# The causal mask of an attention added to the scores by a matrix product instead of a vector addition

## The chip, the core and the metric

The kernel runs on one core of a Trainium2 chip. TensorE is called PE here, VectorE DVE, ScalarE ACT and GpSimd POOL. The metric is the device time of one execution in microseconds; less is better.

## The reference

Four layers, each applied to a layer-normed input and added back: an attention, a gated feed-forward network with integer weights, a state-space layer and a small per-head MLP. The change lies in the attention. It has 2 sequences of 512 tokens, 16 query heads in groups of 4 on 4 key heads, head size 64:

```python
scores = jnp.einsum('bhqd,bhkd->bhqk', q, kg) * scale
causal = jnp.tril(jnp.ones((S, S), dtype=bool))
scores = jnp.where(causal[None, None], scores, jnp.finfo(scores.dtype).min)
attn = jax.nn.softmax(scores, axis=-1)
out = jnp.einsum('bhqk,bhkd->bhqd', attn, vg)
```

## The kernel before

The program is one after the other: `attention`, `feed_forward`, `state_space`, `head_mlp`, each closed by a stage end at which all engines meet. `attention` has three blocks: projections and the first convolution; the second convolution with the rotary embedding; and the block that the change touches, from line 745 on. All its data are fp32.

That last block begins with turning q and k by PE transposes (L763), copied from PSUM by ACT (L838). `k_twice` holds each key head twice, so that `kt` has it on partitions 0 to 63 and again on 64 to 127. A query head h lies in `qt` on partitions 0 to 63 when h is even and on 64 to 127 when it is odd.

Then comes the loop over 32 units (b, z, kv): sequence b, query block z of 128 tokens, counted down from 3 to 0, key head kv. A unit has four heads (GQ = 4), and since later key blocks are masked off its scores have (z + 1) * 128 columns, so 512, 384, 256 or 128. Units 0 to 15 are sequence 0, units 16 to 31 sequence 1. PSUM bank i (0 to 3) holds the scores of head i of the unit, banks 4 and 5 the turned probabilities, bank 6 the value products, bank 7 the output projection.

In step u each engine does this, in the order of its own program:
- PE: `scores(u)`, one product for each of four heads (L775), each after the exponentials of the same head in unit u - 1 have freed the bank (`exp_done`); at odd u `values` for two older units (L798); from u = 7 on a quarter of an output projection (`project`, L815); `turn(u - 1)`, four transposes for each key block of the unit before (L787), where block k waits until ACT has emptied the bank that block k - 2 used (`pt_done`).
- DVE: for each head `top`: wait for the product, add the mask block `neg` in PSUM to the last 128 columns (L868), take the row maximum (L872); and `invert`, the reciprocal of the row sum (L880); then the copies of the value products (L891) and, every fourth step, the layer norm of the projection.
- ACT: four exponentials with row sums (L849), then the copies of the turned probabilities of unit u - 1 (L858).
- POOL: the probabilities times the reciprocal (L922).

`neg` is 128 x 128: 0 on and below the diagonal, -3.0e38 above it. It is loaded in the first block, as `core.ident` is, the identity.

Of the kernel before, what the change touches and what calls it, by code (L numbers as in the profile page):

```python
# [5 lines left out]
ALU = mybir.AluOpType  # L6
ACT = mybir.ActivationFunctionType
AX = mybir.AxisListType
F32 = mybir.dt.float32
F32R = mybir.dt.float32r  # L10
# [3 lines left out]
P = 128  # L14
B, S, D = 2, 512, 512
# [157 lines left out]
def add_vector(dve, core, s, t, src, scaled):  # L173

    dve.bn_stats(core.stats[:, t, :], src).then_inc(s.stats, 1)
    dve.wait_ge(s.stats, t + 1)
    dve.bn_aggr(core.mv[:, t, :], core.stats[:, t, :]).then_inc(s.aggr, 1)
    dve.wait_ge(s.aggr, t + 1)
    dve.tensor_scalar(core.vare[:, t:t + 1], core.mv[:, t, 1:2], LN_EPS, None, ALU.add).then_inc(s.vare, 1)
    dve.wait_ge(s.rstd, t + 1)  # L180
    if t >= 2:
        dve.wait_ge(s.added, t - 1)
    dve.tensor_scalar(scaled[:, t % 2, :], src, core.mv[:, t, 0:1], core.rstd[:, t:t + 1],
                      ALU.subtract, ALU.mult).then_inc(s.scaled, 1)
# [11 lines left out]
def attention(core, x_in, w_qkv, w_o, w_c1q, w_c1k, b_c1, w_c2q, w_c2k, b_c2q, b_c2k, key_temp,  # L196
              c_ident, c_neg, c_sel, c_cos, c_sin):
    nc, ps, x = core.nc, core.ps, core.x
# [4 lines left out]
    with ExitStack() as outer:  # L203
        def keep(name, shape, dt=F32):
            return outer.enter_context(nc.sbuf_tensor(name, shape, dt))
# [4 lines left out]
        neg = keep("neg", [P, P])  # L210


        with ExitStack() as inner:
            def sb(name, shape, dt=F32):
                return inner.enter_context(nc.sbuf_tensor(name, shape, dt))
# [483 lines left out]
        with ExitStack() as inner:  # L699
# [7 lines left out]
            kt = sb("kt", [P, KV0, B * S])  # L707
# [5 lines left out]

            ot = q_tok[:, :, :, :].rearrange("p t h d -> p (t h d)").rearrange("p (f n) -> p f n", f=QT)
            scaled = sb("scaled", [P, 2, D])

            twice_done = core.sem("a_twice_done")
            turn_ready = core.sem("a_turn_ready")
            turn_done = core.sem("a_turn_done")
            sc_ready = core.sem("a_sc_ready")  # L720
            masked = core.sem("a_masked")
            max_done = core.sem("a_max_done")
            exp_done = core.sem("a_exp_done")
            rsum_done = core.sem("a_rsum_done")
# [19 lines left out]
            with nc.Block() as blk:  # L744
# [5 lines left out]
                def _(pe):  # L750
                    for t in range(NT):
                        for j in range(TURNS):
                            n = t * TURNS + j
# [9 lines left out]
                                last = pe.transpose(ps[:, n % 4, i * P:(i + 1) * P], src, core.ident[:, :])  # L763
                            last.then_inc(turn_ready, 1)
                    pe.wait_ge(turn_done, NT * TURNS)

                    def scores(u):
                        b, z, kv = units[u]
                        wide = (z + 1) * P
                        for i in range(GQ):  # L770
                            h = kv * GQ + i
                            at = slice((h % 2) * HD, (h % 2 + 1) * HD)
                            if u >= 1:
                                pe.wait_ge(exp_done, (u - 1) * GQ + i + 1)
                            pe.matmul(ps[:, i, 0:wide], qt[at, h // 2, b * S + z * P:b * S + (z + 1) * P],  # L775
                                      kt[at, kv, b * S:b * S + wide], start=True, stop=True).then_inc(sc_ready, 1)

                    def turn(u):
                        b, z, kv = units[u]
# [49 lines left out]

                @blk.scalar  # L830
                def _(act):
                    for t in range(NT):
                        for j in range(TURNS):
                            n = t * TURNS + j
                            at = t // 2 * 2 * P + t % 2
                            dst = qt[:, 4 * j:4 * j + 4, at:at + 2 * P - 1:2] if j < TURNS - 1 else kt[:, :, t * P:(t + 1) * P]
                            act.wait_ge(turn_ready, n + 1)
                            act.activation(dst, ps[:, n % 4, :].rearrange("p (i n) -> p i n", i=4), ACT.Copy).then_inc(turn_done, 1)  # L838
                    for u in range(NU + 1):
                        if u < NU:  # L840
                            b, z, kv = units[u]
                            wide = (z + 1) * P
                            for i in range(GQ):
                                n = u * GQ + i
                                act.wait_ge(max_done, n + 1)
                                if u >= 2:
                                    act.wait_ge(pt_ready, tiles_before[u - 1])
                                    act.wait_ge(prob_done, n - 2 * GQ + 1)
                                act.activation(prob[:, u % 2, i, 0:wide], ps[:, i, 0:wide], ACT.Exp,  # L849
                                               bias=nmax[:, u % 2, i:i + 1],  # L850
                                               accum_out=psum_row[:, u % 2, i:i + 1]).then_inc(exp_done, 1)
                        if u >= 1:
                            for k in range(units[u - 1][1] + 1):
                                n = tiles_before[u - 1] + k
                                act.wait_ge(pt_ready, n + 1)
                                if u >= 5:
                                    act.wait_ge(pv_ready, (u - 5) // 2 + 1)
                                act.activation(prob_t[:, (u - 1) % 4, k, :, :],  # L858
                                               ps[:, 4 + n % 2, :].rearrange("p (i n) -> p i n", i=GQ), ACT.Copy).then_inc(pt_done, 1)

                @blk.vector
                def _(dve):
                    def top(u, i):
                        b, z, kv = units[u]
                        n = u * GQ + i
                        own = ps[:, i, z * P:(z + 1) * P]
                        dve.wait_ge(sc_ready, n + 1)
                        dve.tensor_tensor(own, own, neg[:, :], ALU.add).then_inc(masked, 1)  # L868
                        dve.wait_ge(masked, n + 1)
                        if u >= 2:  # L870
                            dve.wait_ge(exp_done, n - 2 * GQ + 1)
                        dve.tensor_reduce(nmax[:, u % 2, i:i + 1], ps[:, i, 0:(z + 1) * P], AX.X, ALU.max,  # L872
                                          negate=True).then_inc(max_done, 1)

                    def invert(u, i):
                        n = u * GQ + i
                        dve.wait_ge(exp_done, n + 1)
                        if u >= 2:
                            dve.wait_ge(prob_done, n - 2 * GQ + 1)
                        dve.reciprocal(rsum[:, u % 2, i:i + 1], psum_row[:, u % 2, i:i + 1]).then_inc(rsum_done, 1)  # L880

                    def store(pair):

                        b, z, first_kv = units[2 * pair]
                        t = b * ZB + z
                        dve.wait_ge(pv_ready, pair + 1)
                        for half in range(2):
                            kv = first_kv + half
                            turned = ps[half * HD:(half + 1) * HD, PV_BANK, :].rearrange("p (f e n) -> p f e n", e=2, n=P)
                            for e in range(2):  # L890
                                dve.tensor_copy(ot[e * HD:(e + 1) * HD, kv * (GQ // 2):(kv + 1) * (GQ // 2), t * P:(t + 1) * P],  # L891
                                                turned[:, :, e, :]).then_inc(ot_done, 1)

                    def add(j):
                        t = order[j]
                        dve.wait_ge(wo_ready, j + 1)
                        add_vector(dve, core, ad, j, ps[:, OUT_BANK, :], scaled)

                    for e in range(2):
                        dve.tensor_copy(k_twice[:, :, :, e, :], k_tok[:, :, :, :]).then_inc(twice_done, 1)  # L900
                    for u in range(NU + KV0 + LAG):
                        for i in range(GQ):
                            if u < NU:
                                top(u, i)
                                if i >= 1:
                                    invert(u, i - 1)
                        if u < NU:
                            invert(u, GQ - 1)
                        if u % 2 == 1 and 3 <= u < NU + 3:
                            store((u - 3) // 2)  # L910
                        if u >= KV0 + LAG and (u - KV0 - LAG) % KV0 == KV0 - 1:
                            add((u - KV0 - LAG) // KV0)
# [1452 lines left out]
```

## Time and profile before

| | us |
|---|---|
| median of 3 runs | 2778.62 |
| lowest and highest run | 2778.03, 2780.35 |
| the profiled execution | 2781.88 |
| its span | 2780.1 |
| mean granted clock of TensorE in it | 0.953 of full speed |

| engine | busy us | share of the span |
|---|---|---|
| PE | 2493.9 | 90% |
| DVE | 1750.2 | 63% |
| ACT | 1411.5 | 51% |
| POOL | 1506.0 | 54% |

The loop of the last attention block takes some 228 us of the span, from 468 to 697 us; the state-space layer takes most of the rest. The trace gives an fp32 product as two matmul records and an fp32r product as one. Matmul records overlap when they are pipelined, since each lasts until its result is out, so it is the distance between two starts that tells how long PE is taken up. A time is read from the start of the span.

### The profile page before, as it was taken

What the parts mean: (1) busy time and instruction counts of PE and PEld (TensorE: products, weight loads), DVE (VectorE), ACT (ScalarE), POOL (GpSimd) and SP (SyncE); (2) the same over time, 40 slices, a digit from 0 to 9 for tenths busy, and PEclk for the clock granted to TensorE, in tenths of its full rate; (3) what the DMA queues carried; (4) which work ended last, traced back from release to release, by engine and by line L of the source; (5) the groups of instructions that cost most, each with busy time, mean ns of one, the idle gap of its engine ahead of it and who ended that gap; (6) DMA issues with size and microseconds to landing.
All of it is one profiled execution on the core that took longest, in us unless ns stands there. A gap on an engine that the chain in (4) does not pass through costs nothing. (4 is left out here: it accounts for less than half of the span.)

```text
span 2780.1 us, 37283 instructions
## 1 busy us (share of the span) xinstructions
PE 2493.9 (90%) x12664; PEld 1826.8 (66%) x12664; DVE 1750.2 (63%) x3126; ACT 1411.5 (51%) x2787; POOL 1506.0 (54%) x1291
## 2 busy tenths in 40 slices
PE   7989995898799359999999999999999999999948
PEld 3464443444587247877877877877877877877734
DVE  2153444566423547778778778778777777777764
ACT  2200003554221156766866866866766766766603
POOL 0053465444001026777777777767767767767641
PEclk9999997999899679999999999999999999999978
DMA  4012310000210053334333333333343343343210
GB/s 157 0 56 62 118 47 30 1 1 1 91 39 0 34 181 102 111 114 115 111 114 122 113 116 125 104 115 122 106 124 114 102 131 107 102 136 108 70 46 31
DMA packets 142188, 241.86 MB, mean 87 GB/s; under 512 B 28209, under 2 KB 48433, under 8 KB 141745
## 3 DMA queue, kind: packets, MB, share of 16 engines
q1 hardware_dynamic: 142000, 239.48, 27.7%
q8 instruction: 103, 1.69, 0.3%
q14 instruction: 85, 0.69, 0.1%
HBM read 232.08 MB, written 7.34 MB: 86 GB/s over the span
## 5 line engine op out<-in xcount | busy, mean ns | idle before, releaser
L1646 ACT ACTIVATE mix<-mix,sc 128x128 f32<-128x128 f32 x1024 | 310.8, 389 | 4.4 <-DMA mix<-row_cum 4.4
L96 PE MATMUL ps<-s_xt_hi,w_in_hi 128*128 128x512 f32 x640 | 267.0, 417 | 49.4 <-ACT sg L1638 32.5
L1745 DVE SCALAR_TENSOR_TENSOR feat<-ps,chan,feat 128x511 f32<-128x511 f32 (+2 forms) x384 | 283.9, 739 | 10.0 <-ACT feat L1628 8.2
L1857 POOL TENSOR_TENSOR w_in_lo<-w_in_raw,w_in_hi 128x512 fp32r<-128x512 f32 x160 | 216.6, 1354 | 114.8 <-ACT w_in_hi L1603 114.8
L1775 DVE TENSOR_TENSOR y_lo<-y,y_hi 128x512 fp32r<-128x512 f32 x128 | 171.4, 1339 | 161.5 <-ACT y_hi L1662 159.5
L1734 DVE TENSOR_TENSOR mix<-mix,cb 128x512 f32<-128x512 f32 x256 | 271.0, 1064 | 0.0
L1841 POOL TENSOR_TENSOR xend<-xdt,sc 128x384 f32<-128x384 f32 x128 | 106.9, 835 | 283.8 <-DVE xdt L1708 282.2
L98 PE MATMUL ps<-s_xt_hi,w_in_lo 128*128 128x512 f32 x640 | 253.2, 396 | 0.0
L97 PE MATMUL ps<-s_xt_lo,w_in_hi 128*128 128x512 f32 x640 | 251.8, 394 | 0.0
L96 PE MATMUL ps<-s_xt_hi,w_g_hi 128*128 128x512 f32 x512 | 213.1, 416 | 21.1 <-DVE feat L1745 21.0
L1518 PE MATMUL ps<-w_o_hi,y_hi 128*128 128x512 f32 x512 | 207.4, 405 | 5.4 <-DVE y_lo L1775 3.4
L98 PE MATMUL ps<-s_xt_hi,w_g_lo 128*128 128x512 f32 x512 | 204.0, 398 | 0.0
L1520 PE MATMUL ps<-w_o_hi,y_lo 128*128 128x512 f32 x512 | 203.3, 397 | 0.0
L1519 PE MATMUL ps<-w_o_lo,y_hi 128*128 128x512 f32 x512 | 203.0, 396 | 0.0
L97 PE MATMUL ps<-s_xt_lo,w_g_hi 128*128 128x512 f32 x512 | 201.4, 393 | 0.0
L1853 POOL TENSOR_TENSOR y<-y,sg 128x512 f32<-128x512 f32 x128 | 195.1, 1524 | 10.0
L1862 POOL TENSOR_TENSOR w_g_lo<-w_g_raw,w_g_hi 128x512 fp32r<-128x512 f32 x128 | 199.0, 1555 | 0.0
L1628 ACT ACTIVATE feat<-ps,chan 128x512 f32<-128x512 f32 x128 | 98.4, 769 | 183.1 <-PE ps L98 183.1
L1708 DVE TENSOR_TENSOR xdt<-ps,sc 128x512 f32<-128x512 f32 x128 | 88.1, 688 | 161.1 <-PE ps L1543 160.8
L1874 POOL TENSOR_TENSOR y_sq_sum<-y_sq_sum,y_sq 128x512 f32<-128x512 f32 x112 | 166.8, 1489 | 8.8
L96 PEld LDWEIGHTS ps<-s_xt_hi,w_in_hi 128*128 128x128 f32 x640 | 121.7, 190 | 75.3 <-issue 54.0
L1850 POOL TENSOR_TENSOR y<-y,off 128x384 f32<-128x384 f32 x128 | 129.7, 1013 | 65.3 <-DVE off L1727 65.3
(261 smaller groups left out, 5970.2 us busy)
## 6 DMA issues: line engine op xcount, KB each, us to landing
mix<-row_cum SPq DMA_DIRECT2D x128, 512.0 KB, 5.8
w_in_raw<-in_w_conv_in SPq DMA_DIRECT2D x160, 256.0 KB, 3.2
w_g_raw<-in_w_gate_in SPq DMA_DIRECT2D x128, 256.0 KB, 3.5
ecb<-row_ecum SPq DMA_DIRECT2D x256, 96.0 KB, 3.4
w_o_raw<-in_w_out SPq DMA_DIRECT2D x64, 256.0 KB, 3.0
w<-in_w_c2q SPq DMA_DIRECT2D x16, 768.0 KB, 4.8
w<-in_w_c2q SPq DMA_DIRECT2D x16, 512.0 KB, 3.8
wqkv<-in_w_qkv SPq DMA_DIRECT2D x1, 3072.0 KB, 13.6
```

The lines of the kernel that those rows point to most:

```text
L96: pe.matmul(out, a_hi, b_hi, start=(n == 0), stop=False)
L97: pe.matmul(out, a_hi, b_lo, start=False, stop=False)
L98: last = pe.matmul(out, a_lo, b_hi, start=False, stop=(n == len(terms) - 1))
L1518: pe.matmul(ps[:, OUT + z, :], a_hi, w_o_hi[:, i, :], start=(i == 0), stop=False)
L1519: pe.matmul(ps[:, OUT + z, :], a_hi, w_o_lo[:, i, :], start=False, stop=False)
L1520: last = pe.matmul(ps[:, OUT + z, :], a_lo, w_o_hi[:, i, :], start=False, stop=(i == GT - 1))
L1646: last = act.activation(m, m, ACT.Relu, bias=sc[:, b, CUM, z, 2 * i + e:2 * i + e + 1], scale=-1.0)
L1734: last = dve.tensor_tensor(m, m, cb[:, :], ALU.mult)
L1745: dve.scalar_tensor_tensor(out=to, in0=ps[:, j % 2, 0:S - back], scalar=chan[:, bb % B, j, K1 - 1 - back:K1 - back], in1=to, op0=ALU.mult, ...
L1853: pool.tensor_tensor(yt, yt, sg[:, gate_at(g, bb, i), :], ALU.mult).then_inc(s["y_done"], 1)
L1857: pool.tensor_tensor(w_in_lo[:, n % RING, :, :], w_in_raw[:, n % RING, :, :], w_in_hi[:, n % RING, :, :].bitcast(F32), ALU.subtract).then_ ...
L1862: pool.tensor_tensor(w_g_lo[:, i % RING, :, :], w_g_raw[:, i % RING, :, :], w_g_hi[:, i % RING, :, :].bitcast(F32), ALU.subtract).then_inc ...
```

## The change

The mask is no longer added by DVE. Each score product is left open (`stop=False`), and a second product, identity times mask block, is accumulated on its last 128 columns. Both its operands are fp32r copies, made by ACT at the start of the block. DVE's addition, its semaphore `masked` and the wait on it go; DVE takes the maximum when the mask product is done. PE waits once for the two copies.

```diff
+            neg_r = sb("neg_r", [P, P], F32R)
+            ident_r = sb("ident_r", [P, P], F32R)
+            mask_ready = core.sem("a_mask_ready")
-            masked = core.sem("a_masked")
@@ PE, before the loop
                     pe.wait_ge(turn_done, NT * TURNS)
+                    pe.wait_ge(mask_ready, 2)
@@ PE, scores(u), for each head i
                             pe.matmul(ps[:, i, 0:wide], qt[at, h // 2, b * S + z * P:b * S + (z + 1) * P],
-                                      kt[at, kv, b * S:b * S + wide], start=True, stop=True).then_inc(sc_ready, 1)
+                                      kt[at, kv, b * S:b * S + wide], start=True, stop=False)
+                            pe.matmul(ps[:, i, z * P:(z + 1) * P], ident_r[:, :], neg_r[:, :],
+                                      start=False, stop=True).then_inc(sc_ready, 1)
@@ ACT, at the start of the block
+                    act.activation(neg_r[:, :], neg[:, :], ACT.Copy).then_inc(mask_ready, 1)
+                    act.activation(ident_r[:, :], core.ident[:, :], ACT.Copy).then_inc(mask_ready, 1)
@@ DVE, top(u, i)
-                        own = ps[:, i, z * P:(z + 1) * P]
                         dve.wait_ge(sc_ready, n + 1)
-                        dve.tensor_tensor(own, own, neg[:, :], ALU.add).then_inc(masked, 1)
-                        dve.wait_ge(masked, n + 1)
```

## Rows read from the trace of the kernel before

**Rows 1.** Stretches, all engines: busy us and instructions each, PEclk, DMA share, GB/s.
```profile
468.00:575.00 107.00, 89.47 (x396) 44.81 (x397) 65.46 (x223) 59.91 (x167) 48.37 (x66) 0.89 0.00 1
575.00:682.00 107.00, 97.45 (x449) 48.53 (x449) 74.92 (x249) 61.85 (x172) 53.57 (x74) 1.00 0.00 1
```

**Rows 2.** Groups by line and shape, 468 to 697 us: busy us, mean ns, idle before.
```profile
L868 DVE TENSOR_TENSOR ps<-ps,neg 128x128 f32<-128x128 f32 x128 | 36.6, 286 | 52.0 <-PE ps L775 51.8
```

**Rows 3.** PE's waits, 468 to 697 us: us in total, times, longest.
```profile
PE ps L787 <- ACT prob_t L858: 19.8, 16, 3.2
PE ps L815 <- DVE scaled L183: 5.0, 3, 2.8
```

**Rows 4.** Timeline of PE alone: start us, lasting us, what, idle before it.
```profile
471.64 4.04 PE L775 MATMUL ps<-kt,qt 64*128 64x512 f32 x8 [1.06 <-ACT prob L849]
...
481.80 3.79 PE L775 MATMUL ps<-kt,qt 64*128 64x512 f32 x8
...
579.27 3.94 PE L775 MATMUL ps<-kt,qt 64*128 64x512 f32 x8
...
588.50 1.99 PE L775 MATMUL ps<-kt,qt 64*128 64x512 f32 x8
...
594.96 1.14 PE L787 MATMUL ps<-ident,prob 128*128 128x128 f32 x8 [1.69 <-ACT prob_t L858]
...
604.64 1.15 PE L787 MATMUL ps<-ident,prob 128*128 128x128 f32 x8 [0.25 <-ACT prob_t L858]
605.72 1.56 PE L775 MATMUL ps<-kt,qt 64*128 64x384 f32 x8
...
660.94 0.84 PE L775 MATMUL ps<-kt,qt 64*128 64x128 f32 x4
...
663.64 1.94 PE L798 MATMUL ps<-prob_t,v_tok 128*64 128x512 f32 x8 [0.58 <-ACT prob_t L858]
```

**Rows 5.** Timeline of DVE and ACT in unit 18, and ACT's first copy of the block.
```profile
453.97 0.65 ACT L838 ACTIVATE qt<-ps 128x512 f32<-128x512 f32 x1 [12.87 <-PE ps L763]
...
589.65 0.30 DVE L868 TENSOR_TENSOR ps<-ps,neg 128x128 f32<-128x128 f32 x1 [0.90 <-PE ps L775]
589.99 0.69 DVE L872 TENSOR_REDUCE nmax<-ps 128x1 f32<-128x512 f32 x1
...
590.71 0.69 ACT L849 ACTIVATE prob<-ps,nmax 128x512 f32<-128x512 f32 x1 [1.51 <-DVE nmax L872]
...
593.64 0.69 ACT L849 ACTIVATE prob<-ps,nmax 128x512 f32<-128x512 f32 x1 [0.21 <-DVE nmax L872]
...
594.32 1.08 ACT L858 ACTIVATE prob_t<-ps 128x512 f32<-128x512 f32 x2
```

**Rows 6.** Timeline of PE and its weight loads (PEld) in short windows of unit 18.
```profile
588.29 0.27 PE L787 MATMUL ps<-ident,prob 128*128 128x128 f32 x1
588.50 0.70 PE L775 MATMUL ps<-kt,qt 64*128 64x512 f32 x2
588.49 0.30 PEld L775 LDWEIGHTS ps<-kt,qt 64*128 64x128 f32 x4 [0.17 <-issue]
589.03 0.19 PEld L775 LDWEIGHTS ps<-kt,qt 64*128 64x128 f32 x2 [0.24 <-issue]
589.46 0.19 PEld L775 LDWEIGHTS ps<-kt,qt 64*128 64x128 f32 x2 [0.24 <-issue]
...
590.41 0.30 PEld L815 LDWEIGHTS ps<-wo,q_tok 128*128 128x128 f32 x2 [0.76 <-issue]
590.95 0.19 PEld L815 LDWEIGHTS ps<-wo,q_tok 128*128 128x128 f32 x1 [0.24 <-issue]
```

**Rows 7.** Timeline of PE, fp32r products of 512 columns in the feed-forward layer.
```profile
780.12 0.39 PE L97 MATMUL ps<-f_xt_lo,f_w_hi 128*128 128x512 f32 x1
780.35 0.39 PE L98 MATMUL ps<-f_xt_hi,f_w_lo 128*128 128x512 f32 x1
```

**Rows 8.** A stretch in batch 0, columns as in rows 1.
```profile
481.80:485.50 3.70, 3.70 (x9) 1.18 (x8) 1.52 (x4) 1.13 (x2) 0.00 (x0) 0.50 0.00 0
```

## The prediction, made before the change was run

> **What bounds the kernel now.** I read the table of stretches first, then the groups of the attention loop, then the timeline of TensorE (PE) and the waits. The softmax loop of the attention runs from about 468 to 697 us of a span of 2780.1 us; the change touches nothing after it. In its first half, batch 0, PE is busy 89.5 of 107 us at a mean clock of 0.89; in its second half, batch 1, 97.5 of 107 us at full clock [rows 1]. DVE is busy 65 and 75 us. So PE is nearly the bound in batch 1, and DVE's addition, 36.6 us in all [rows 2], is not work that all runs on the path. The loop has 32 units (2 batches, 4 query blocks, 4 key heads), each with 4 heads. A unit on PE is: score products; in some units value products; in most an output projection part; then the turning of the previous unit's probabilities. The third turn (k=2) needs PSUM bank 4 back, which ACT empties only after the four exponentials of the present unit. Where that chain (scores, addition, maximum, exponential, four times, then the copy) is longer than PE's own work, PE stands still in front of L787: 19.8 us in 16 waits [rows 3]. In unit 18 (batch 1, four key blocks) it is the 1.69 us before 594.96 [rows 4]. The chain there: addition at 589.65, maximum 0.34 later, first exponential at 590.71, the fourth at 593.64, copy at 594.32, turn at 594.96 [rows 4, 5]. In units with value products the wait is 0.25 us, the mere exchange of two banks (the unit that ends at 605.72) [rows 4].
>
> **How the score products run now.** This is what the change meets. A head's product uses 64 rows of the array, the even heads rows 0 to 63, the odd ones 64 to 127. An fp32 product is two passes. At 588.50 two matmuls begin together and last 0.70 us as a pair, with four weight loads beside them; the next pairs begin at 589.03 and 589.46 [rows 6]. So two heads run at the same time, a pass of 512 columns taking 0.43 us for both, and four heads take 1.91 us (588.50 to 590.41) where one after another they would take eight passes, 3.4 us. For 384 columns the eight recorded passes last 1.56 us against 1.99 [rows 4]; the four pairs save 0.43 us, a pass 0.107 per 128 columns. So a pass takes 0.32, 0.215 and 0.11 us for 384, 256 and 128 columns.
> The same rows price a switch between 64-row and 128-row products. The last pass begins at 589.89 (0.43 after 589.46), the projection's first load at 590.41: 0.52 and not 0.43. Its next load but one comes 0.54 later, again 0.11 too much. PE's weight port sat idle 0.76 us on "issue" before it [rows 6]. The way in is alike: transpose at 588.29, scores at 588.50 (0.21, where a transpose pass is 0.11: eight last 1.14 at 594.96, less 0.27 for the last and 0.10 for the opening load, by seven [rows 4]), the second pass 0.53 later. Both ways the extra is 0.10 + 0.10 = 0.20 us, made of a drain and a weight load that is not hidden.
> The page "TensorEngine Tiling (Array Packing)" of the Trainium skill, section Key Properties, says that changing the tiling mode drains TensorE; the trace agrees with 0.20 us. Without such a drain, by the order of the products alone, the sum below would be half of the switches lower, some 20 us.
>
> **The change, part by part.**
> 1. *Removed:* 128 additions on DVE, 0.286 us each [rows 2], and their wait. Worth at most 0.34 us in front of a unit's first maximum, and about 0.25 per further head where DVE paces (four exponentials from 590.71 to 593.64 are about 1.0 apart, of which ACT itself needs 0.68: from 593.64 to the copy at 594.32) [rows 5].
> 2. *Added on PE:* 128 products identity x mask, 128 rows, 128 columns, between the products of two heads. No row shows an fp32r product of 128 columns. A pass of 512 fp32r columns starts every 0.23 us [rows 7], a quarter of which is 0.057; the transposes of the same shape in fp32 take the 0.11 a pass of above, 0.22 for both. I take m = 0.11, the same shape, and keep 0.057 and 0.22 as ends.
> 3. *Changed by it:* the order is now head 0 (rows 0 to 63), mask (all rows), head 1 (rows 64 to 127), mask. PE runs its products in order, and the mask product holds all rows, so head 1 cannot run beside head 0. The scores stretch becomes 8 passes one after another, 4 m, 7 switches of 0.20 and the opening load 0.10. For 512 columns: 3.43 + 0.44 + 1.37 + 0.10 = 5.34 us, where 1.91 was: +3.43. For 384, 256, 128 columns by the same sum: +3.00, +2.57, +2.14. Eight units of each: +89 us of PE time.
> 4. *What of this PE's idle time takes up.*
> (a) Before L787: 19.8 us. The new chain for 512 columns without projection: the last mask product begins 5.23 after the unit's start and is recorded for 0.27 like a transpose [rows 6], so it ends at 5.50; then come maximum to exponential 0.72, exponential to copy 0.68, copy to turn 0.64 [rows 4, 5]. That is 7.54, where PE is free at 5.34 + 0.97 (eight transpose passes of 0.11 and the half switch); so 1.2 us stay idle in two early units, an estimated 1.0 in two of 384 columns, whose maximum and exponential are shorter, and 0.25 in eleven or twelve others. 7.5 stay, 12.3 are taken up.
> (b) PE's other waits, which now lie behind the longer scores stretch: 1.1 us before 471.64 and 2.1 in the 4.04 there, 2.0 in the 3.94 at 579.27 (score products that wait for the exponentials of the unit before); in each batch's unit like that at 660.94, whose value products begin 2.7 us later where 0.64 would do, 2.1, twice [rows 4]; two of the three waits for DVE in front of L815, 2.2 [rows 3]; and an estimated 1.5 of small ones beside them. Together 13.1.
> (c) The clock. In batch 0 it was at 1.2 GHz of 2.4 in several stretches, after PE had stood up to 3.2 us [rows 3]; there the score products last 3.79 us at 481.80 instead of 1.99 [rows 4, 8]. By the stretches this costs about 10 us. With the change the early gaps are 1.0 to 1.2 us, like the 1.69 us of unit 18, after which the clock stayed up. I take it that most of it goes.
> Sum: 89 - 12.3 - 13.1 = 63.6 with the clock as it was, 53.6 with it up all the way. I take +55, near the second.
> 5. *Two ACT copies and two waits* at the loop's front: ACT stands idle 12.87 us before its first copy at 453.97 [rows 5], and each new one has a quarter of that copy's columns and so takes no more than its 0.65 us. Nothing; at most 1.3 us if that cover were gone. The removed semaphore frees nothing else. What follows the loop (feed-forward, state space) is fenced off by a stage end and only starts later.
> Sum against the profiled execution: 2781.9 (span 2780.1 and 1.8 around it) + 55 = 2837. The median of the runs is 3.3 us lower, so 2778.6 + 55 = 2834.
>
> **Rivals.**
> A. *Pairs survive and no switch is paid* (the other side). If PE can load the identity beside running 64-row products and still start head 1 at once, only m is added. Chain-bound units gain 1.1 us at 512 columns, 1.0 at 384, 0.6 at 256: some 11 us over about a dozen units; each head in the 15 PE-bound units costs m, and once in the others: 11.2 - 70 m. That is -7 us (2772) at m = 0.057, -3.5 at 0.11, zero at 0.16, +4 at 0.22. It needs weights to pass from one mode to the other without the 0.76 us that the weight port idles [rows 6], so little speaks for it.
> B. *The clock falls instead.* In the new scores stretch the array streams only 0.97 of 1.37 us per head at 512 columns, 0.33 of 0.72 at 128, half of the rows at a time. If that holds the clock at 1.2 GHz as idle time did in batch 0, the 10 us stay and each added 3.0 to 3.4 us in some seven early units doubles: 63.6 + 21, with m at its upper end + 12: up to +97, 2875.
> C. *The switch costs half:* only the load, not the drain, since the mask needs no data from outside. 7 x 0.10 x some 28 units = 20 us less, with the small m 6 less: +27 to +35, 2806 to 2814.
> D. *The change does nothing measurable:* DVE's addition is hidden and so is the product. It would need case A with m near 0.11 to 0.2.
>
> **How the numbers follow.** Forecast (about +40 to +75) 0.70; B 0.15; C 0.08; A and D together 0.07, of which 0.03 faster by over 0.2% (5.6 us, about what a measurement can tell from no change) and 0.04 within it. Slower by more: 0.93. Ends of m alone move the sum by -6 and +12 us, the clock by -2 and +8. The range goes from C's 2805 to 2880, just beyond B, and leaves out A and D and some of B.
>
> **What the profile would show.** Right: L775's two heads no longer begin together; the stretch from a unit's first score product to the next other work is about 5.3 us at 512 columns and 2.8 at 128; PEld idles on "issue" twice per head; the wait of L787 for ACT shrinks to some 8 us; ACT's exponentials are spaced 1.3 to 1.4 us at 512 columns instead of 1.0; DVE waits longer for PE. Batch 1, 575 to 682 us before, takes 34 us more; batch 0 some 20 more; everything after is only moved. Wrong: score products still beginning in pairs (A), a mean clock below 0.89 in the loop (B), switches of 0.1 us (C), or a stretch that differs because a 128-column fp32r product is nearer 0.06 or 0.22 than 0.11.

## The result, and the profile after

| | us |
|---|---|
| before, median of 5 runs | 2779.63 (2778.03 to 2780.93) |
| after, median of 5 runs | 2860.53 (2839.75 to 2863.03) |
| ratio | 1.0276 (95% interval 1.0241 to 1.0312) |
| the profiled execution after, and its span | 2839.75, 2837.9 |
| mean granted clock in it, and in the other four | 0.954, and 0.943 to 0.945 |

The change makes the kernel 2.8% slower, 81 us, where 55 were forecast, with a range up to 2880 us. The profiled execution is the fastest of the five, 21 us below their median, so the profile after shows less than the median costs.

The table of stretches, for batch 0 (first score product of unit 0 to that of unit 16) and 15 units of batch 1 (unit 16 to unit 31), columns as in rows 1; here and below these stretches begin up to 0.4 us behind the product itself. In the kernel before:

```profile
468.59:575.00 106.41, 89.46 (x396) 44.80 (x397) 65.46 (x223) 59.37 (x165) 48.37 (x66) 0.89 0.00 1
575.00:670.86 95.86, 88.28 (x415) 44.13 (x414) 67.57 (x224) 58.00 (x160) 49.39 (x66) 1.00 0.00 1
```

In the changed kernel:

```profile
468.54:600.71 132.17, 127.74 (x461) 62.18 (x461) 52.49 (x164) 60.01 (x167) 49.21 (x68) 0.91 0.00 1
600.71:735.58 134.87, 132.86 (x474) 63.44 (x473) 53.56 (x161) 59.20 (x160) 49.58 (x66) 0.94 0.00 1
```

PE is busy 128 and 133 us instead of 89 and 88, DVE 52 and 54 instead of 65 and 68. DVE was relieved of 13 or 14 us in each, and PE took on 38 and 45. The timeline of PE alone shows how, in a unit of 512 columns (unit 19, with value products and a projection part):

```profile
629.29 1.12 PE L778 MATMUL ps<-kt,qt 64*128 64x512 f32 x2
630.34 0.33 PE L780 MATMUL ps<-neg_r,ident_r 128*128 128x128 f32 x1
630.60 1.12 PE L778 MATMUL ps<-kt,qt 64*128 64x512 f32 x2
631.65 0.33 PE L780 MATMUL ps<-neg_r,ident_r 128*128 128x128 f32 x1
631.90 1.12 PE L778 MATMUL ps<-kt,qt 64*128 64x512 f32 x2
632.96 0.33 PE L780 MATMUL ps<-neg_r,ident_r 128*128 128x128 f32 x1
633.21 1.12 PE L778 MATMUL ps<-kt,qt 64*128 64x512 f32 x2
634.27 0.33 PE L780 MATMUL ps<-neg_r,ident_r 128*128 128x128 f32 x1
634.52 3.65 PE L803 MATMUL ps<-prob_t,v_tok 128*64 128x512 f32 x16
```

Before, one row held the eight passes of all heads in 1.99 us [rows 4], two heads side by side [rows 6]. Now each head stands alone: two passes, mask product, 1.31 us later the next head, and 5.23 us until the value products where it was 1.92 in the same unit. The weight loads (PEld) of the same unit say what stands between:

```profile
630.34 0.19 PEld L780 LDWEIGHTS ps<-neg_r,ident_r 128*128 128x128 f32 x1 [0.76 <-issue]
630.60 0.29 PEld L778 LDWEIGHTS ps<-kt,qt 64*128 64x128 f32 x2
631.65 0.19 PEld L780 LDWEIGHTS ps<-neg_r,ident_r 128*128 128x128 f32 x1 [0.76 <-issue]
```

The idle weight port in front of a load, 0.76 us on "issue", is the one that stood in front of L815 in unit 18 [rows 6], once per unit, behind its score products. Now it stands in front of each mask product: in these rows the identity is loaded only when the mask product begins, not beside the 64-row products before it. ACT paces with PE, no longer with DVE; the exponentials of unit 18 are 1.31 us apart, from 1.00:

```profile
622.15 0.69 ACT L856 ACTIVATE prob<-ps,nmax 128x512 f32<-128x512 f32 x1 [1.44 <-DVE nmax L876]
...
623.46 0.69 ACT L856 ACTIVATE prob<-ps,nmax 128x512 f32<-128x512 f32 x1 [0.53 <-DVE nmax L876]
...
624.78 0.69 ACT L856 ACTIVATE prob<-ps,nmax 128x512 f32<-128x512 f32 x1 [0.53 <-DVE nmax L876]
```

The waits, all engines (who waited for whom, us in total, times, longest), show DVE's maximum waiting for PE 120 us in all; PE's wait for ACT is down from 19.8 us [rows 3] to 6.4:

```profile
DVE nmax L876 <- PE ps L780: 120.3, 113, 14.9
...
PE ps L792 <- ACT prob_t L865: 6.4, 16, 1.2
```

### The profile page after: what moved, and what is told of

Same layout as the page of the kernel before. It is cut to its first block and busy times, and to the rows that moved or that the text cites. A ratio compares the mean times of both kernels' runs of the same rounds, so it can differ in the third digit from the quotient of the medians.

```text
span 2837.9 us, 37414 instructions
## 1 busy us (share of the span) xinstructions
PE 2571.2 (91%) x12792; PEld 1860.2 (66%) x12792; DVE 1721.4 (61%) x2998; ACT 1413.4 (50%) x2789; POOL 1506.7 (53%) x1291
## 5 line engine op out<-in xcount | busy, mean ns | idle before, releaser
L926 POOL TENSOR_TENSOR prob<-prob,rsum 128x512 f32<-128x512 f32 (+3 forms) x128 | 91.3, 719 | 174.0 <-DVE rsum L884 173.1
```

## The experiments

In the runs below the kernel before was run beside each; its median there was 2775.7 to 2776.8 us. The diffs are against the changed kernel unless said, and shortened. The granted clock has two levels here, 1.00 and half of it; "at half clock" is the time at the lower one, which is twice what is missing to 1.00 in a stretch's mean, times its length.

### Where the changed kernel's scatter comes from: `again` and `again2`

No edit.

> The changed kernel once more, unchanged. Its profiled execution took 2839.75 us, the four others 2857 to 2863, and their mean granted clock was 0.944 instead of 0.954. Theory: the work on every engine is the same, and the 20 us are stretches at 1.2 GHz; a profile near 2860 us then shows the same distances of 1.31 us between two heads of 512 columns wherever the clock is up, and more stretches at half clock than the 41 us in the attention loop of the first profile. Rival: a wait or a transfer differs; then the clock is 0.954 again in a profile near 2860 us and some line's wait is longer by 20 us.

> One more look at the changed kernel. Two profiled executions so far: 2839.75 us with 41 us of the attention loop at 1.2 GHz, and 2850.3 us with 65 us of it there, everything else alike: 24 us more at half clock cost 10.6 us. If the clock is the whole of the scatter, an execution of 2860 us has 85 to 90 us of the loop at half clock and the same distance of 1.31 us between heads of 512 columns wherever the clock is up.

Measured: 2859.3 us (2850.3 to 2876.1, 4 runs; ratio 1.0305, 1.0266 to 1.0344), profile with a span of 2848.5; then one execution of 2867.33 us, span 2865.5. Its two stretches, same columns and units as above:

```profile
468.72:624.00 155.28, 152.76 (x461) 72.42 (x460) 52.72 (x164) 60.55 (x167) 49.24 (x68) 0.75 0.00 1
624.00:755.15 131.15, 129.40 (x475) 63.23 (x473) 53.66 (x162) 59.16 (x160) 49.57 (x66) 0.96 0.00 1
```

The numbers of records are the same but for one; the clock is 0.75 in batch 0 instead of 0.91. Half-clock time in these stretches: 41, 65 and 89 us in the three profiles, and the attention ends (first transpose of the feed-forward) at 773.8, 783.9 and 793.2 us: 10 us for each 24 us at half clock. Inside such a stretch the timeline of PE reads:

```profile
488.31 2.07 PE L778 MATMUL ps<-kt,qt 64*128 64x512 f32 x2
490.32 0.47 PE L780 MATMUL ps<-neg_r,ident_r 128*128 128x128 f32 x1
490.72 2.07 PE L778 MATMUL ps<-kt,qt 64*128 64x512 f32 x2
```

2.41 us from head to head at 1.2 GHz where it is 1.31 at 2.4 GHz. The first theory holds. No profile was taken at the median of 2860.53 us. That execution's mean clock of 0.944 over 2858.7 us is 320 us at half clock, and in the three profiles 222 to 243 us of such time lay outside the loop; so an estimated 75 to 100 us lay in it, where the kernel before had 24.

In the kernel before, the early falls of the clock, at 478.9, 489.2, 506.2 and 519.9 us, each came with a wait of PE of 2.5 to 3.2 us. In the changed kernel PE had not stood idle: in the first profile the clock fell at 475.4 us, in the middle of the score products of unit 1, with no wait since the loop began at 468.3:

```profile
474.61 0.33 PE L780 MATMUL ps<-neg_r,ident_r 128*128 128x128 f32 x1
474.87 1.56 PE L778 MATMUL ps<-kt,qt 64*128 64x512 f32 x2
476.35 0.47 PE L780 MATMUL ps<-neg_r,ident_r 128*128 128x128 f32 x1
476.75 2.07 PE L778 MATMUL ps<-kt,qt 64*128 64x512 f32 x2
```

### Four heads, then four masks: `four_then_masks`

```diff
-for i in range(GQ): product(i); mask(i).then_inc(sc_ready, 1)
+for i in range(GQ): product(i)
+for i in range(GQ): mask(i).then_inc(sc_ready, 1)
```

> The changed kernel with the same four mask products, moved behind the four score products of the unit. Theory (broken pairs and switches are the cost): the score products begin in pairs again, one switch per unit is left, so a unit's scores stretch is some 0.4 us longer than before the change and not 3.4 us (512 columns) to 2.1 us (128); the time is 2780 to 2795 us. Rival (the mask product itself costs, or accumulating into the bank that was just written): the stretch keeps 2 us or more of the added time and the kernel stays above 2820 us.

Measured: 2777.85 us, ratio to before 1.0002 (0.9992 to 1.0011). The same four products cost 81 us in one order and in the other no more than what leaving out DVE's addition gives back. PE's timeline in unit 18:

```profile
589.37 1.99 PE L779 MATMUL ps<-kt,qt 64*128 64x512 f32 x8
591.29 0.66 PE L782 MATMUL ps<-neg_r,ident_r 128*128 128x128 f32 x4
591.79 1.93 PE L822 MATMUL ps<-wo,q_tok 128*128 128x512 f32 x4
```

The 1.99 us of eight paired passes are back [rows 4], and the masks take 0.50 us until the projection. In units that PE bounds, each is 0.45 to 0.59 us longer than before. The time is 2 us below the foot of what I had written: units whose chain over DVE and ACT ends last got shorter, units 17 and 29 by 0.98 and 1.46 us.

### Two heads, then two masks: `two_then_masks`

> The mask products behind each pair of heads: pairs of score products are kept, three switches per unit instead of seven. Theory (each switch costs 0.20 us): 0.4 us per unit more PE time than with one switch, so the stretch is 0.8 us longer than before the change; a first head that is ready about 1 us earlier than with all four in front gives some of it back. 2785 to 2800 us. If the loss of the pairs alone made the cost and the switches were free, this one would be no slower than with one switch; if the switches alone made it and pairs were worth nothing, it would be 3/7 of the way, some 2805 to 2815 us.

Measured: 2773.76 us, ratio 0.9993 (0.9982 to 1.0005): no difference that can be measured, and 11 us below the least I had expected. PE's timeline in unit 19:

```profile
588.00 1.13 PE L779 MATMUL ps<-kt,qt 64*128 64x512 f32 x4
589.06 0.44 PE L782 MATMUL ps<-neg_r,ident_r 128*128 128x128 f32 x2
589.43 1.13 PE L779 MATMUL ps<-kt,qt 64*128 64x512 f32 x4
590.49 0.44 PE L782 MATMUL ps<-neg_r,ident_r 128*128 128x128 f32 x2
590.86 3.65 PE L805 MATMUL ps<-prob_t,v_tok 128*64 128x512 f32 x16
```

2.86 us for the scores instead of 1.92: +0.94, which is 0.35 more than with all four masks at the end (+0.59 in this unit). So two further switches cost 0.35, 0.17 each. The PE time was right; the total was not, because the first batch is 6 us shorter than before (100.2 against 106.4): its early chains are shorter and the clock is 0.97 there instead of 0.89, 7 us at half clock instead of 24. By the rate above these 17 us are worth 7, so without the clock the batch would be no shorter.

### No mask at all: `no_mask`

The kernel before without DVE's addition; the mask is left out of the computation altogether.

> The kernel before without DVE's addition and without any mask product, so the mask is left out altogether and the softmax runs over all columns of the unit. It bounds what DVE's addition costs. Theory (the addition lies on the path only where the chain of maxima and exponentials sets the pace): 8 to 14 us faster than before, near 2768 us, almost all of it in units without value products. Rival (the addition is hidden everywhere): within 2 us of before. Rival (it is on the path in all 128 heads): 30 us or more faster.

Measured: 2756.15 us, ratio 0.9926 (0.991 to 0.9942): 20.7 us, half as much again as the upper end of what I expected. Unit by unit, batch 1 with unit 31 is 8.8 us shorter, all in nine units (2.0 in unit 17, 0.95 in 18, 20 and 22, 1.8 in unit 29) and 0.0 in each unit that PE bounds, so the place was right. Batch 0 is 15 us shorter, of which some 7 are the clock (0.96 instead of 0.89, 17 us less at half clock). Without the clock that is 8 to 9 us in each batch.

### All 128 rows for the scores: `full_rows`

```diff
-pe.matmul(..., qt[at, h // 2, ...], kt[at, kv, ...], start=True, stop=False)
+pe.matmul(..., qt[:, h // 2, ...], kt[:, h % 2, kv, ...], start=True, stop=False)
```

`kt` is held twice, with zeros set by POOL on the 64 partitions that a head doesn't have, and ACT writes it in two copies per tile; `prob` shares its memory with `k_twice` to make room.

> The changed kernel with its order (product, mask, product, mask), but the score products use all 128 rows: the keys are held twice, once with zeros on the lower and once on the upper 64 partitions, so no product has 64 rows and no switch takes place; the pairs are as lost as in the changed kernel. It separates the two costs. Theory (7 switches of 0.20 us and 4 passes per unit, both real): a unit's scores stretch is 3.9 us at 512 columns instead of 5.2, 1.3 us less per unit; 30 to 45 us faster than the changed kernel, 2800 to 2825 us. If the switches were the whole cost: 2785 us or less. If the lost pairs were: no faster than the changed kernel. On the clock: if it is the gaps of the switches that let it fall, the loop's share at 1.2 GHz goes back to the 24 us of the kernel before or less; if it is products without a partner as such, it stays at 40 to 90 us.

Measured: 2791.49 us, ratio 1.0048 (1.0028 to 1.0067). PE's timeline:

```profile
490.88 1.02 PE L780 MATMUL ps<-kt,qt 128*128 128x512 f32 x2
491.34 0.62 PE L782 MATMUL ps<-neg_r,ident_r 128*128 128x128 f32 x1
491.80 1.07 PE L780 MATMUL ps<-kt,qt 128*128 128x512 f32 x2
492.31 0.63 PE L782 MATMUL ps<-neg_r,ident_r 128*128 128x128 f32 x1
492.77 1.07 PE L780 MATMUL ps<-kt,qt 128*128 128x512 f32 x2
```

The order and the lost pairs are those of the changed kernel, the distance is 0.97 us instead of 1.31: two passes of 0.43 and 0.11. So the two switches take 0.34 us of each head beyond that, 1.3 us of a unit, and the lost pairs 0.43 x 2 x 2 = 1.7 us at 512 columns. The kernel is 8 us below the foot of the forecast, though its loop begins 11.5 us later (479.8 instead of 468.3, the doubled copies of ACT); apart from that it would be some 3 us above the kernel before. Its loop is at full clock all the way, in both batches. It keeps the lost pairs and costs far less than 81 us, so they alone don't make it. No run has all seven switches and the pairs as well; by the times of a unit both cost, and the clock comes on top.

### The mask product as fp32: `fp32_mask`

```diff
-neg_r = sb("neg_r", [P, P], F32R)
-ident_r = sb("ident_r", [P, P], F32R)
+neg_r = sb("neg_r", [P, P])
+ident_r = sb("ident_r", [P, P])
```

> The changed kernel with identity and mask block as fp32 instead of fp32r: two passes of 128 columns for each mask product. The distance between two heads of 512 columns in the changed kernel is 1.31 us = 2 passes of 0.43, two switches of 0.20 and 0.06 for the mask. Theory: fp32 makes it 0.21, so 0.15 us more per head, 0.6 per unit, 15 to 20 us in all. Rival (the time of so small a product is not its columns but its load and its way through the array): within 5 us of the changed kernel.

Measured: 2842.2 us, ratio 1.0231 (1.021 to 1.0252), 17 us faster than with fp32r, against both expectations. PE's timeline:

```profile
619.24 1.12 PE L778 MATMUL ps<-kt,qt 64*128 64x512 f32 x2
620.29 0.49 PE L780 MATMUL ps<-neg_r,ident_r 128*128 128x128 f32 x2
620.71 1.12 PE L778 MATMUL ps<-kt,qt 64*128 64x512 f32 x2
```

1.47 us from head to head, 0.16 more than with fp32r: the size of the product was as expected. But the granted clock is 1.00 in both batches:

```profile
468.16:600.31 132.15, 126.80 (x525) 65.74 (x525) 52.73 (x164) 59.87 (x167) 49.28 (x68) 1.00 0.00 1
600.31:736.18 135.87, 133.87 (x533) 67.73 (x533) 53.61 (x161) 59.18 (x160) 49.65 (x66) 1.00 0.00 1
```

The attention ends at 773.4 us, as in the best profile with fp32r (773.8), which had 41 us at half clock. The other three executions have a higher mean clock (0.960 to 0.962) than the profiled one (0.958). PE still waits in front of L792 as in the first profile after, 1.21 us in each of two early units of 512 columns where that one has 1.18, so waits of this length do not by themselves bring the clock down.

### 64-row mask products: `half_rows`

```diff
+for part in range(2):
+    for i in range(first, first + 2):
+        rows = ...            # lower half for one head, upper for the other, then exchanged
+        if part == 1: pe.wait_ge(half_done, u * GQ + first + 2)
+        pe.matmul(..., ident_r[rows, :], neg_r[rows, :], start=False, stop=(part == 1))
```

> The mask products as 64-row products too: each is cut into the upper and the lower half of identity and mask block, and two heads take turns on the two halves of the array, the second half product of a head after a wait for the first. No switch of the array's form within the scores at all, pairs are kept. Theory (switches cost, pairs matter): a unit's scores stretch is longer than before the change only by the half products and the wait, some 1.0 us, and DVE's addition is gone: 2765 to 2785 us, about as with two switches more (2773.8 us). Rival (the wait between the halves costs more than the switches it saves): 2790 us or more.

Measured: 2776.93 us, ratio 1.0002 (0.999 to 1.0014). A unit that PE bounds is 1.01 us longer than before, as forecast, where `two_then_masks` is 0.79 to 0.94 longer. The four half products of a pair take 0.88 us in its timeline (592.08 to 592.96), two whole ones with their two switches 0.37 (589.06 to 589.43 above). That the wait for PE's own result eats what the missing switches give is the likely reason; no view names this wait.

### A second fp32r product: `twice_r`

> The changed kernel with a second fp32r product per head, identity times a block of zeros, in front of the mask product: the same work twice, its result unchanged. It asks why the clock falls in the changed kernel (41, 65 and 89 us of the attention loop at 1.2 GHz in three profiles, the slower the more) and does not fall at all with the mask as fp32 (0 us), although that one keeps PE waiting just as often. With the second product the distance between two heads of 512 columns should be 1.37 to 1.42 us, near the 1.47 us of fp32. Theory (the share of time in which the array streams decides): few or no stretches at 1.2 GHz, 2835 to 2850 us, so more work and yet faster than the changed kernel's 2859 us. Rival (fp32r products count for less than fp32 ones, or the form does): the clock falls as in the changed kernel, and the time is 2865 to 2880 us.

Measured: 2867.72 us, ratio 1.0325 (1.0302 to 1.0348). The second product adds 0.11 us per head (1.42 from head to head), and the clock falls as before, 65 us of the loop at half clock. That is the rival's outcome, but the run doesn't test the theory: if 128 columns stream in 0.057 us [rows 7], only half of the 0.11 us added is streaming, and the share of time in which the array streams does not rise.

### DVE's addition kept: `both`

> The changed kernel with DVE's addition and its wait put back, and the mask product kept in place but with zeros for the mask block, so that the mask is added once and by DVE. It says what the removal of the addition brings in the changed kernel. Theory (PE spaces the heads by 1.31 us, more than the 1.0 us of addition and maximum, so the addition lies beside PE's work): nothing per unit wherever PE has the projection or the value products to do, 0.3 us in each of the four units of the first batch in which the chain still ends last; 1 to 2 us in all with the clock left aside. Rival: the removal brought the 20 us that leaving the mask out brings in the kernel before; then 2875 us or more.

Measured: 2864.21 us, ratio 1.0308 (1.0292 to 1.0324); the changed kernel was at 1.0305. Against the first profile after, twelve of the sixteen units of batch 1 differ by 0.00 to 0.04 us each, and unit 4 by the 0.33 of one addition. The other four of batch 1 lie at other clocks. Beside PE's 1.31 us per head the addition costs nothing in these twelve: the removed work had left the path.

### Products only where the chain ends last: `hybrid` and `hybrid_b`

```diff
+by_pe = u % 16 in (1, 2, 4, 6, 13, 15)      # PE: mask products behind each pair, else none
+if not by_pe: dve.tensor_tensor(own, own, neg[:, :], ALU.add).then_inc(masked, 1)
```

> Mask products behind each pair of heads only in the units where the chain over DVE and ACT ends last (units 1, 2, 4, 6, 13 and 15 of each sequence), DVE's addition in all others. By the unit times of the run with masks behind each pair against the kernel before: 8.2 us less in those units of batch 0, 4.2 less in batch 1, and none of the 0.8 to 0.9 us more in each of the others. Theory: 2765 to 2772 us, 0.2 to 0.5% faster than before. Rival (the gain of batch 0 was the clock's, which stayed up because PE was busier everywhere): 2773 to 2777 us, no difference.

> As the run before it, with units 5 and 7 of batch 0 as well. With masks behind each pair these two were 0.5 and 1.5 us faster than before, but the same units of batch 1 were 0.9 us slower each, so what they gained in batch 0 was the clock. Theory (the clock is up anyway once the gaps of units 1 to 6 are gone): about 1.5 us slower than without them. Rival (their additional products are what keeps the clock up): 2 to 4 us faster than without them.

Measured: 2765.46 us, ratio 0.9961 (0.9947 to 0.9974); and with units 5 and 7 of batch 0 added 2767.52 us, ratio 0.9971 (0.996 to 0.9982). The first is faster than both kernels of this case, 10 us below the one before beside it. Its stretches of batch 0 and of 15 units of batch 1:

```profile
467.59:562.83 95.24, 84.36 (x422) 44.23 (x420) 59.94 (x202) 58.58 (x167) 48.70 (x68) 0.98 0.00 1
562.83:657.04 94.21, 90.98 (x436) 46.45 (x432) 62.02 (x202) 57.12 (x160) 48.41 (x65) 1.00 0.00 1
```

Batch 0 takes 95.2 us instead of 106.4 and its clock is 0.98 instead of 0.89 [rows 1]: 3 us at half clock instead of 24, some 8 to 9 of the 11 us. Batch 1 gains 1.7 us, and unit 31 gives 1.4 of them back. With the pairs kept, the clock stays up once the gaps of the early units are short. The two variants' intervals overlap; that the second is slower isn't shown.

## Why the prediction was right, and where it was off

The measured 2860.53 us lie in the range up to 2880, but outside the +40 to +75 us that I gave 0.70: 81 is what rival B describes. The place and the work were right, the course of the clock was not.

**The place and the mechanism on PE** were right. Score products no longer begin together, seven switches stand in a unit, the wait for ACT in front of L787 goes from 19.8 to 6.4 us (8 were forecast), and DVE's addition is worth nothing here where it can be compared (`both`). One sign was off: PEld idles on "issue" once per head, not twice. The rule of the page "TensorEngine Tiling (Array Packing)" of the Trainium skill, section Key Properties, that a change of the tiling mode drains TensorE, agrees with `full_rows`: with the mode kept, 0.34 us per head less.

**The terms, at full clock:**

| step | forecast | measured |
|---|---|---|
| 512 columns, scores stretch | 5.34 us | 5.23 and 5.15 us (units 19, 18) |
| head to head, 512 columns | 1.37 us | 1.31 us |
| mask product and its two switches | 0.11 + 0.40 us | 1.31 - 0.86 = 0.45 us |
| a unit bound by PE, 256 columns | +2.57 us | +2.46 and +2.33 us (units 25, 26) |
| a unit bound by PE, 128 columns | +2.14 us | +1.90 us (unit 30) |
| unit 17, with the waits it takes up | 3.43 - 2.0 - 0.17 = +1.26 us | +1.21 us |
| unit 24, with the wait it takes up | 2.57 - 0.64 = +1.93 us | +1.68 us |

The two forecasts for units 17 and 24 are worked out from the prediction's terms afterwards; 0.17 is that unit's 0.42 us in front of L787 less the 0.25 that stay.

Of the 0.45 us, the mask product itself takes some 0.05. `fp32_mask` shows this: its two mask passes reach from 620.29 to 620.71, 0.42 us, which less two passes of 0.107 leaves 0.20 for the switches there; in the changed kernel the one fp32r pass with the same switches is 630.34 to 630.60, 0.26. So it has the price of 128 columns at 512 columns' rate, the lower end [rows 7], not that of the transposes. With four products in some 28 units, m was 6 us too high, the smaller error. Behind another 128-row product it takes 0.11 us (`full_rows`, `twice_r`). That its own load shows there, and lies within the switch in the changed kernel, is how I read it; no run separates the two.

**The step that failed is 4(c), the clock.** I took off 10 us, because the long gaps of batch 0 would go. They went (the longest left is 1.18 us where it was 3.2, and 1.2 was forecast), but the clock fell all the same: 41, 65 and 89 us of the loop at half clock instead of 24, and in batch 1 as well, where it had been up throughout. The mean clock of the loop is 0.92, 0.88 and 0.85 in the three profiles; the prediction had named a mean below 0.89 as the sign of B. Going by 10 us for each 24 us, the first profile's attention, which ends 64.9 us later than before, is 48 + 17: 48 us of work, which is the 53.6 forecast at full clock less 6 for m, and 17 for the clock. `fp32_mask` says the same in another way: its loop is at full clock and its attention ends 64.5 us later than before, of which its longer mask products are some 18 to 20 (0.16 us each), which leaves 45 to 47 of work. At the median 81 - 48 = 33 us are left for the clock and for what the later stages vary by. So the forecast was 6 us too high in the work and some 30 too low in the clock. B had priced the clock at 31 us (10 that stay and 21 more), so its mechanism came at about its full price, though without the dearer mask product that it added for its upper end. I had given it 0.15. That the profiled execution lies 58 us above the profile before, near the 55 forecast, is luck: 6 us less work, 17 for the clock and 7 less in the stages behind cancel. The gaps in front of L787 bear on the clock while the pairs are kept (`two_then_masks`, `hybrid`); with the pairs broken they were not what mattered.

**What rule sets the clock stays open.** It fell in the order product, mask as fp32r, with 7 switches per unit (`again`, `again2`, `both`), and with a second fp32r product (`twice_r`). It stayed at 1.00 with the mask as fp32 and the same switches (`fp32_mask`), and without switches (`full_rows`). With the same fp32r products behind pairs or behind all four heads it stayed at 1.00 in batch 1 (`two_then_masks`, `four_then_masks`). So neither the fp32r form alone nor the switches alone bring it down. The page "TensorE: Matmul & The Clock Gate" of the Trainium skill, section The HAM clock gate, ties the clock to how busy PE has been. By the records PE was busy 152.8 of 155.3 us in the slowest stretch and 126.8 of 132.2 with the mask as fp32, where the clock stayed up, so busy time as the profile counts it doesn't tell these apart. Whether the form of the products or the share of time in which data streams decides wasn't separated.

**The rivals.** A (pairs survive, no switch) did not come: the pairs break and 0.34 us of switches stand in each head. Its gain from shorter chains was put at 11 us; `no_mask` shows 8.8 in batch 1 alone, some 17 in both, and 20.7 in all with the clock. C (0.10 us for a switch) is refuted: 0.34 us for two. D needed A.

Later stages are not touched, but not equal either: the state-space layer took 1775.6 us before and 1769.2, 1769.5 and 1778.9 in the three profiles after, at a mean granted clock of 0.96 before and 0.97, 0.97 and 0.96 after. The feed-forward took 0.8 us less in the first than before. That is why that profile's span is 57.8 us longer when its attention ends 64.9 later. Why these stages vary stays open.

## What to carry to other kernels

Before putting a product between others on PE, look which rows they use: if two products of 64 rows run side by side, one that takes all rows splits them and costs a switch each way, here 3.3 us in a unit of 512 columns for 0.2 us of work; behind the group it costs 0.45 to 0.59 us per unit. A step moved from an engine that isn't the bound to one that nearly is pays only in the units where the chain through it ends last, and the trace's waits name those units. Where PE's clock has two levels, a change that makes it work with small breaks has to be forecast with and without it, and timed in more than one execution.

## What I had not expected of the hardware

- An fp32r product of 128 columns adds some 0.05 us of PE between two switches, no more per column than one of 512 (0.23 us), but 0.11 us behind another 128-row product.
- The clock fell in stretches in which PE was busy 98% of the time by the records, to 0.75 over 155 us. The ten executions of the changed kernel lie between 2839.75 and 2876.08 us; in the three that were profiled most of the difference is the clock in the attention.
- The same work with the mask in fp32, 0.16 us more per head, ran at full clock throughout and was faster: 1.0231 against 1.0305 times the kernel before.
